# A four-layer graph network on one core: the order of instructions in two attentions is changed

## The reference, cut to what matters

```python
x = x + elu(softmax_over_rows(where(adj > 0, leaky_relu(f1[i] + f2[j]), NEG)) @ h)  # first attention, h = LN(x) @ W
x = x + mixture_of_8_experts_top2(LN(x))                                          # gelu experts
x = x + softmax(where(adj == k, leaky_relu((hidden * a_k) @ hidden.T), NEG)) @ hidden  # edge attention, hidden = LN(x)
x = x + dense_mixture_of_8_experts(LN(x))                                         # two relu layers
```

## Time and profile before

| what | value |
|---|---|
| three runs | 1122.26, 1122.6, 1124.46 us; median 1122.6 |
| the profiled execution | 1122.47 us, span 1120.7 us |
| TensorE busy | 1038.0 us (93%), mean granted clock 0.985 |
| ScalarE busy | 771.2 us (69%) |
| VectorE busy | 679.2 us (61%) |
| GpSimd busy | 384.4 us (34%) |
| first attention | from about 22 to 290 us of the span |
| edge attention | from about 464 to 768 us |

### The profile page before, as it was taken

One profiled execution on the slowest core, in us unless ns is written; L12 is line 12 of the kernel. 1 busy time (PEld: TensorE's weight loads), 2 busy tenths in 40 slices (PEclk: granted clock), 3 DMA queues, 4 the chain that ended last, 5 costly groups with the idle time before them and its releaser, 6 DMA issues. The chain is left out here.

```text
span 1120.7 us, 19950 instructions
## 1 busy us (share of the span) xinstructions
PE 1038.0 (93%) x6440; PEld 744.8 (66%) x6481; DVE 679.2 (61%) x2122; ACT 771.2 (69%) x1155; POOL 384.4 (34%) x468
## 2 busy tenths in 40 slices
PE   4888888798899999689999999999999999999998
PEld 4555555465477777478888878886466666666667
DVE  5688899778544345378988899863533333233336
ACT  5998889776565554478888888885666655655561
POOL 4123778877572504446565654111000000000000
PEclk9999999999899999899999999999999999999999
DMA  8978998713256764323333222210000000000001
GB/s 308 354 267 289 365 339 294 268 58 113 72 185 217 205 192 147 96 65 88 84 88 88 84 82 76 57 39 1 1 1 20 10 10 20 10 10 20 10 13 36
DMA packets 69145, 131.15 MB, mean 117 GB/s; under 512 B 9918, under 2 KB 30764, under 8 KB 68012
## 3 DMA queue, kind: packets, MB, share of 16 engines
q1 hardware_dynamic: 60268, 111.96, 29.4%
q0 software_dynamic: 8192, 16.79, 5.1%
q10 hardware_dynamic: 576, 1.05, 0.3%
HBM read 77.60 MB, written 52.17 MB: 116 GB/s over the span
## 5 line engine op out<-in xcount | busy, mean ns | idle before, releaser
L2346 PEld LDWEIGHTS eY<-Vo,dGW 128*128 128x128 f32 x1024 | 132.4, 191 | 54.1 <-issue 52.8
L541 POOL DMA_INDIRECT sorted_x<-V,AT_I x128 | 125.6, 981 | 57.5 <-issue 37.4
L730 PE MATMUL O<-Y,HS 128*128 128x512 f32 x256 | 129.6, 627 | 10.7 <-DVE Vo L1117 10.7
L2346 PE MATMUL eY<-Vo,dGW 128*128 128x128 f32 x1024 | 134.2, 276 | 0.1
L2329 PE MATMUL eU<-XTN,V 128*128 128x512 f32 x256 | 130.9, 593 | 0.9 <-PEq L2264 0.9
L2337 PE MATMUL eU<-H,V 128*128 128x512 f32 x256 | 131.1, 594 | 0.0
L2516 DVE TENSOR_TENSOR dGW<-H,WBC 128x512 f32<-128x512 f32 x80 | 55.3, 692 | 124.9 <-PE eY L2346 124.8
L1947 POOL DMA_INDIRECT W<-sorted_y,ROW_I x96 | 97.4, 1015 | 79.2 <-PE f_T L2021 29.7
L2048 PEld LDWEIGHTS f_O<-f_XN,f_PT 128*128 128x128 f32 x896 | 105.6, 192 | 20.7 <-DVE X L2159 18.3
L2425 ACT ACTIVATE H<-eU,bn 128x512 f32<-128x512 f32 x128 | 99.5, 777 | 25.5 <-PE eU L2329 16.2
L2048 PE MATMUL f_O<-f_XN,f_PT 128*128 128x128 f32 x896 | 111.6, 278 | 5.7 <-DVE X L2159 4.1
(11 more groups left out here) (306 smaller groups left out, 2048.9 us busy)
## 6 DMA issues: line engine op xcount, KB each, us to landing
XTN<-in_adj SPq DMA_DIRECT2D x64, 512.0 KB, 7.2
masks<-NMW SPq DMA_DIRECT2D x8, 2048.0 KB
f_MK<-masks SPq DMA_DIRECT2D x60, 256.0 KB, 2.8
sorted_y<-zero SPq DMA_DIRECT2D x39, 256.0 KB
NMW<-sorted_x SPq DMA_DIRECT2D x39, 256.0 KB, 2.7
sorted_y<-NMW SPq DMA_DIRECT2D x39, 256.0 KB, 2.6
X<-in_x SPq DMA_DIRECT2D x8, 512.0 KB, 7.6
out_x<-X SPq DMA_DIRECT2D x16, 256.0 KB, 2.3
```

Of the source, the lines that this page charges most:

```text
L541: g_.indirect_dma_start(sorted_x, bass.IndirectOffsetOnAxis(ap=AT_I[b % 2][:, kt:kt + 1], axis=0), XR[b % 2][:, t * P:(t + 1) * P], None). ...
L730: pe.matmul(O[:, h * HALF:(h + 1) * HALF], HS[:, g % 3, :], Y[:, g % 4, h * HALF:(h + 1) * HALF], start=False, stop=(c == NT - 1)).then_in ...
L2346: i = pe.matmul(Y[q][:, t * P:(t + 1) * P], GW[:, j % 2, t * P:(t + 1) * P], Vo[:, e * P:(e + 1) * P], start=(e == 0 and t == 0), stop=(e ...
```

## The change

Six places. In the first attention: TensorE's projection of the next batch, pieces 0 and 1, moves in column 2 from ahead of `attend` to behind it (batch 0 keeps the old order); ScalarE's two row copies in column 1 move ahead of the exponential of the tile before; VectorE's first four conversions of the next mask move from the end of column 2 to column 3, behind `elu`, `shift` and `share` and ahead of `seat` (again not in batch 0). In the edge attention ScalarE's rectifier and the second raw copy of tile g move ahead of the exponential of tile g - 1. No instruction is added or removed.

```diff
@@ -745,7 +745,7 @@
                     if c == 1 and b < LAST:
                         for h in range(2):
                             turn_x(b + 1, h)
-                    if c == 2 and b < LAST:
+                    if c == 2 and b == 0:
                         for k in range(2):
                             project(b + 1, k)
                     if c == 3 and b < LAST:
@@ -765,6 +765,9 @@
                         pe.transpose(M[1][:, 0:R], prow[:, :], ident[0:R, 0:R]).then_inc(pcol_step, 1)
                     if g >= 3:
                         attend(g - 3)
+                    if c == 2 and 1 <= b < LAST:
+                        for k in range(2):
+                            project(b + 1, k)
                     if c == 0 and b >= LAST - 1:
                         rank(b - 2)
                     if b == LAST and c == 1:
@@ -954,13 +957,13 @@
                     if c == 3 and b >= 1:
                         grown(b - 1)
                     relu(g)
+                    if c == 1 and b < LAST:
+                        for h in range(2):
+                            copy_xnt(b + 1, h)
                     if g >= 1:
                         prob(g - 1)
                     if c == 0 and b >= 2:
                         weight(b - 2)
-                    if c == 1 and b < LAST:
-                        for h in range(2):
-                            copy_xnt(b + 1, h)
                     if c == 2 and b < LAST:
                         for k in range(2):
                             copy_h(b + 1, k)
@@ -1299,6 +1302,9 @@
                     shift(g)
                     if g >= 1:
                         share(g - 1)
+                    if c == 3 and 1 <= b < LAST:
+                        for t in range(4):
+                            convert(b + 1, t)
                     if c == (3 if late_rank(b) else 0) and b >= 2:
                         seat(b - 2)
                         if b == LAST:
@@ -1324,7 +1330,7 @@
                     if c == 6 and b < LAST:
                         copy_f1(b + 1)
                     if b < LAST:
-                        for t in (((), (), (), (0, 1), (2, 3), (4, 5), (6, 7), ()) if b == 0 else ((), (), (0, 1, 2, 3), (), (), (4, 5), (6, 7), ()))[c]:
+                        for t in (((), (), (), (0, 1), (2, 3), (4, 5), (6, 7), ()) if b == 0 else ((), (), (), (), (), (4, 5), (6, 7), ()))[c]:
                             convert(b + 1, t)
                     if c == 6 and b >= 1:
                         choose_first(b - 1)
@@ -2112,10 +2118,10 @@
                 for g in range(G):
                     own, after = turn_at(g // NT, g % NT)
                     keep_raw(g, 0)
+                    relu(g)
+                    keep_raw(g, 1)
                     if g >= 1:
                         prob(g - 1)
-                    relu(g)
-                    keep_raw(g, 1)
                     if own:
                         copy_turned(own)
                     if g >= 2:
```

## The result

| what | before | after |
|---|---|---|
| median of runs (us) | 1123.14 (5 runs, 1122.26 to 1124.46) | 1115.47 (5 runs, 1113.22 to 1117.33) |
| ratio after/before | | 0.9924, interval 0.9912 to 0.9936 |
| the profiled execution's span | 1120.7 | 1112.1 |
| first block load of the expert stage | 283.39 | 285.04 |
| first scores of the edge attention | 461.91 | 462.89 |

The change took 7.7 us by the medians; the forecast said 7.5. The ratio in the table, 0.9924, is not that of the two medians (0.9932); by it the change took 8.5 us. In the profiled executions it is 8.6, and the stages part it: up to the edge attention the changed kernel is 0.98 us *behind*, in the edge attention it gains 9.6 us. The forecast had -0.1 and -7.65, so the sum agrees better than its terms.

The account below looks back on a forecast made before the run. It took a VectorE-TensorE-ScalarE chain to bound the first attention and TensorE the edge attention. From 1122.5 us, -0.1 (first attention: -1.8 and +1.7) and -7.65 (edge attention) gave 1114.8, said as 1115; range 1111 to 1121.

Parts of the forecast that it names:

- the middle: Edge attention: waits for normalised rows (2.1) and for X (1.7) shrink; together 3.8 us, bounds 0 and 6.1.
- part 4: Edge attention, all 64 tiles: the rectifier moves ahead of the exponential; 7.65 us won in all.
- part 3: First attention, four conversions moved from column 2 to column 3: elu 0.47 us earlier, 0.46 per batch, bounds 0 and 1.4.
- start, to the tile of the weighted copy: Edge attention's first tiles: rectifier and raw copy come earlier until TensorE bounds from tile 4; 2.4 us, at most 4.7.
- the wait for the weighted copy: Edge attention, batch 1: a 2.3 us wait; the rectifier could have started 0.85 us earlier, so 0.85 won.
- part 1: First attention, column 1: row copies ahead of the exponential make VectorE's share of column 0 later by 0.94 us, bounds nothing to 0.94.
- Part 2: First attention, column 2: projection behind the product finishes logits of column 3 about 1.6 us earlier; worth nothing by itself.
- 2.5 lies between: First attention, merged 2.5 us pause: between 2.01 (clock stayed) and 2.81 (fell); one of three batches pays 1.7 us.
- A: First attention: the clock falls in each merged pause, stage +3.3 instead of -0.1, 1118.2 us; chance 0.14.
- B: Edge attention gives nothing but 1 us for the start, as TensorE is the bound; 1121.4 us; chance 0.12.
- C: Edge attention: a closed ring through ScalarE, each of 64 tiles paying 0.2 us more, +12.8, 1135 us; chance 0.09.
- D: The clock never falls in the first attention, and the edge attention's middle gives 5.1 instead of 3.8: 1111.7 us; chance 0.09.

Follow-up runs that it names:

- the first and third group: Sets of follow-up kernels sharing runs of the kernel before: 1124.32 us in the first, 1123.22 in the third; the second met a slower chip, 1187.14.
- the first-attention kernel: The kernel before with only the three reorders of the first attention, edge attention as before: 1124.77 us, ratio 1.0002.
- kernel with the filled pause: The whole change, with the four matmuls of the projection's last piece done three times ahead of the elu: ratio 0.9904, then 1112.05 us, ratio 0.9895.

## Why the prediction was right

The result lay 0.5 us from the forecast, but by errors of both signs, which is luck: the edge attention gave 9.6 instead of 7.65, the stages up to it +1.0 instead of -0.1. Two steps of the forecast failed, the size of the middle in part 4 and, in part 3, that a later `seat` holds up nobody but the sends.

**Part 4, by its terms** (starts of the turn of probabilities, from which both traces give all 64 tiles):

| term | forecast | measured |
|---|---|---|
| start, to the tile of the weighted copy | 2.4 | 2.2 |
| the wait for the weighted copy | 0.85 | 0.7 |
| middle | 3.8 | 6.3 |
| end | 0.6 | 0.5 |

The start is 497.19 to 496.00, 1.19 us, and the 0.98 by which the stage began later. The middle is the term that was mis-sized. Four of its batches took 37.3 to 37.4 us before and 36.3 after, 1.0 to 1.1 each, where the forecast had 0.76. The wait for normalised rows gave back 0.30 (forecast 0.36), the wait for X 0.34 (0.4). The rest, 0.47 per batch, is in three tiles in which no row has a bracket: 0.07, 0.18 and 0.22 us. One such tile in the kernel before, with VectorE's addition into X, and TensorE in the same tile of the changed one:

```profile
643.86 0.35 DVE L2159 SCALAR_TENSOR_TENSOR X<-f_O,f_RZ,X 128x128 f32<-128x128 f32 x1
643.93 0.38 PE L2021 MATMUL f_T<-f_MK,identb 128*128 128x512 bf16 x1
644.27 2.05 PE L2048 MATMUL f_O<-f_XN,f_PT 128*128 128x128 f32 x16
```

```profile
638.85 0.38 PE L2027 MATMUL f_T<-f_MK,identb 128*128 128x512 bf16 x1
639.06 1.95 PE L2054 MATMUL f_O<-f_XN,f_PT 128*128 128x128 f32 x16
```

From the mask product to the product it is 0.34 us and 0.21, from there to the turn of the probabilities (646.16 before, 640.85 after) 1.89 and 1.79. It is the wait for X again: the addition ends at 643.86 + 0.35 = 644.21, and the product starts 0.05 behind it, at 644.27. No bracket is printed, because the mask product's modelled end (643.93 + 0.38) lies behind the product's start. In the changed kernel the addition is over at 638.51, 0.55 us ahead of the product. The products of the two other tiles start 0.05 and 0.08 us behind an addition in the kernel before, and 0.32 and 0.18 in the changed one. So the wait for X gave back not 0.4 but about 0.8 us per batch. I had bounded the middle by the printed waits at 6.1, and the truth is just outside: rows without a bracket are not rows without a wait. It is found by setting the distance of two starts beside the shortest distance of the same pair.

**Parts 1 and 3** came out as written, within 0.2 us, as far as column 4 and where the clock stayed up: share 0.93 later, elu 0.3 to 0.5 earlier, rectifier of column 4 as much. Behind column 4 part 3 failed. It counted 0.46 us each for batches 3 and 4 because the shift of column 4 "has slack to the next rectifier" and the seat numbers were only due at the sends. Measured: 0.08 us won in batch 3 and 0.22 lost in batch 4, because TensorE's turn of the elu waits for `seat` (0.22 and 0.35 us printed). That bracket (0.22 to 0.67 us) stands in batches 3 and 4 of the changed kernel's trace and of each in the first and third group that has the conversions moved, except in the three batches that lost the clock at the elu, and not in the edge reorder alone. Also, the 0.94 that part 1 puts on the share takes two thirds of the 1.41 that part 3 wins. The forecast wrote this down and didn't ask what part 3 gives without part 1: 1.4 us at the elu, and a kernel faster by 0.005 of its time.

**Part 2** was priced at nothing for itself and at 1.7 per clock fall, with falls in one of three batches. Measured: falls in two of four in the changed kernel, in three of four in the first-attention kernel, each at 1.3 to 1.8 us (table below), so the price was right and the number by chance higher. In batch 2 the wait for fresh entries of `adj` swallowed it, as was said: 113.91 had 1.77 us of idleness and the same look has none after, and from +2.5 us at column 4 of batch 2 the delay fell to +0.7 at column 1 of batch 3. The stage lost 1.0 us to the edge attention and 1.65 to the first block load, in one execution: at column 1 of batch 6 the delay was 0.65 us, and batch 6 then took 37.57 us against 35.96, but it took 34.25 in the edge reorder alone, whose first attention is that of the kernel before. So one trace doesn't settle this sum to within a microsecond or two; by the ratios it is 0.2 us alone and 2.5 as the difference between the whole change and the edge reorder. The forecast's own range for it was -1.8 to +3.3.

**The clock.** Behind pauses at the copied rows and at the elu, in batches 1 to 4 of the traces of the first and third group and of before and after, the clock fell after 1.88, 1.97, 1.98, 2.03, 2.06 (twice), 2.22, 2.31, 2.32, 2.40, 2.53, 2.54 and 2.69 us, and not after 1.98, 2.07, 2.12, 2.13, 2.33, 2.50, 2.54 (twice) and 2.71. It fell behind none of 1.82 and less there. The cost is read from executions of one and the same order, that of the changed kernel (its own trace, its repetition in batches 1 and 2, the first-attention kernel and the kernel with the raw copy behind). From the rectifier of column 1 to that of column 4, in us:

| | batch 1 | batch 2 | batch 3 | batch 4 |
|---|---|---|---|---|
| kernel before | 12.27 | 12.79 | 12.83 | 12.83 |
| changed order, clock kept | 11.87 | 12.36, 12.36 | 12.35, 12.53 | 12.53, 12.36 |
| changed order, clock fell | 13.20, 13.24, 13.54 | 14.02, 14.02 | 14.03 | 14.18 |

With the clock kept the order wins 0.3 to 0.5 us at column 4, as forecast; a fall costs 1.3 to 1.8 us more. The kernel with the filled pause has 11.88, 12.36, 12.37 and 12.55, the numbers of the second row. This shows that the falls, and not the order, make the changed kernel's batches 1 and 2 slower than before. That a shorter pause makes falls rarer rests on the counts: 13 in 22 pauses against none in 23 of 1.08 to 1.82 us.

So the forecast's step "2.5 lies between" took a chance for a border: the rows 2.01 (no fall) and 2.81 (fall) couldn't tell that either may go the other way next time. The Trainium skill, page "TensorE: Matmul & The Clock Gate", section "HAM oscillation", has the loop fall back at each long pause. Its own case has longer pauses than these 22; the traces agree for a longer one here, TensorE's wait for the first loaded block (4.19 to 4.80 us), at which the clock fell in all ten traces of the kernel before, the changed one and the first and third group. Around 2 us the "each" doesn't carry over: 13 falls in 22 pauses from 1.88 us up.

**The rivals.** A (falls in each merged pause, 1118.2) didn't come; the projection alone came near to its time (0.9955), though its trace has no fall behind 2.60 us. B (the edge attention gives nothing) is excluded by the edge reorder alone. C, a ring through ScalarE, is not what the change does, but the raw copy behind the exponential is a near relative: it puts work of ScalarE between the rectifier and VectorE's shift, and the 14 us against the changed kernel are 0.22 for each of 64 tiles. D's middle (5.1) was nearer to the truth than mine.

**A table of the first attention's parts**, each with conversions and edge attention moved (ratio to the kernel before; the pause is TensorE's longest of the two in batches 1 to 4):

| | projection as before | projection behind the product |
|---|---|---|
| copies as before | 0.9874 (1.4 to 2.1 us) | 0.9874 (1.3 to 1.7 us) |
| copies ahead | 0.9889 (1.8 to 2.3 us) | 0.9924 (2.0 to 2.5 us) |

The changed kernel is the slowest corner of the four. By the middle values each single move costs at most 0.0015; together they cost 0.005, about 5.6 us, more than the sum. The three others lie within each other's intervals, and more than one group of runs stands behind the table, so no order among them is shown.

## What to carry to other kernels

On an in-order engine, put the work that starts the next tile ahead of the work that ends the last one, as long as the latter has slack, and move all of it that another engine waits for (here rectifier and raw copy together). Ask of each piece moved later who waits for what now stands behind it: the conversions ahead of `seat` made TensorE wait and took back 0.4 to 0.5 us per batch. Read what a move does to the length of single pauses of an engine with a granted clock, not only to their sum. And time the parts of a change apart: two that cost at most 0.0015 each cost 0.005 together, hidden by the edge attention's reorder that gave 11 us.

## What the runs showed of the hardware

- The granted clock after a pause of about 2 us is not a function of the pause's length: the same order of instructions read 1.00 in one execution after 1.98 us and 0.5 in another after 1.97.
- A fall of the granted clock cost 1.3 to 1.8 us each, in executions of one order with and without it.
- TensorE's work of 0.95 us more per batch, in a pause, came with a kernel about 3 us faster (0.9895 against 0.9924, intervals that just touch; 0.9904 against 0.9926 on one chip, intervals that overlap).
- One chip ran all kernels 5 to 6% slower than the others, 1187.14 us for the kernel before. Its traces have idle times of one to nine microseconds of several engines that name no releaser. Their cause stays open.
